# Five rotating banks, an earlier place for the routing matmuls and nine lead units in a routed feed-forward kernel

## What is computed

```python
idx, w = _route(xf, Wr, br)                      # 6 of 32 experts per row, weights w
gate = jnp.zeros((T, E), w.dtype).at[jnp.arange(T)[:, None], idx].add(w)

def step(acc, ew):
    w1, w2, g = ew
    h = jnp.square(jax.nn.relu(xf @ w1.T)) @ w2.T
    return (acc + g[:, None] * h, None)
acc, _ = jax.lax.scan(step, jnp.zeros_like(xf), (W1, W2, gate.T))
shared = jnp.square(jax.nn.relu(hidden_tensor @ Ws1.T)) @ Ws2.T
return shared + moe_out
...
x = x + s * g                                    # g = silu(shared + moe_out)
```

## Time and profile before

| | |
|---|---|
| median of three timed runs | 337.94 us (333.05, 337.94, 338.01) |
| profiled execution | 335.13 us, span 333.3 us |
| TensorE busy | 297.5 us, 89% of the span |
| VectorE, ScalarE, GpSimd busy | 229.0, 179.3, 208.0 us |
| mean granted TensorE clock | 0.968 of full speed |
| gathers of rows, issue to landing, median | 3.3 us |
| gathers of slots' results | 66 by 0.98 us |

### The profile page before, as it was taken

The page is one execution under the profiler, slowest core; times in us unless marked ns, Lnnn a source line. Parts: engine busy times, 40 slices in busy tenths (PEclk is TensorE's granted clock), DMA queues, the critical chain, the costliest instruction groups (busy, mean ns, idle before and its releaser), DMA issues.

```text
span 333.3 us, 6927 instructions
## 1 busy us (share of the span) xinstructions
PE 297.5 (89%) x2224; PEld 231.8 (70%) x2224; DVE 229.0 (69%) x585; ACT 179.3 (54%) x293; POOL 208.0 (62%) x226
## 2 busy tenths in 40 slices
PE   0577899879997999999999999998999999995994
PEld 0344666547776977888888698885767767785893
DVE  3788678887631378677778767687767576753774
ACT  3888598695452755557665576653363331212322
POOL 1874656681577777777777777304666777774640
PEclk9997899989997999999999999999999999995999
DMA  7455746722463376676766767555688777666552
GB/s 283 188 176 190 239 146 244 283 94 63 104 180 116 108 222 204 201 204 207 219 203 194 219 196 210 183 173 192 181 327 259 220 197 212 189 182 163 147 154 79
DMA packets 39651, 62.92 MB, mean 189 GB/s; under 512 B 5282, under 2 KB 25538, under 8 KB 39618
## 3 DMA queue, kind: packets, MB, share of 16 engines
q1 hardware_dynamic: 31794, 41.11, 37.2%
q0 software_dynamic: 7824, 21.38, 23.4%
HBM read 46.13 MB, written 16.33 MB: 187 GB/s over the span
## 4 chain that ended last, share of the span: by engine, by line
PE 56%; DMA 15%; POOL 8%; DVE 7%; ACT 6%; issue 6%; DVEq 1%; ACTq 0%
PE rot L962 12%; PE dp L990 10%; DMA yk<-ytab,slot 10%; PE rot L915 5%; PE hp L939 4%; DMA xgt<-xtab,ids 4%; POOL xgt L614 4%; PE hp L951 3%; PE hp L953 3%; PE hp L952 3%; POOL yk L623 3%; PE hp L941 3%; PE hp L940 3%; PE rot L975 2%; DVE xs L1265 2%
## 5 line engine op out<-in xcount | busy, mean ns | idle before, releaser
L614 POOL DMA_INDIRECT xgt<-xtab,ids x97 | 96.4, 994 | 39.7 <-issue 21.3
L680 ACT ACTIVATE hf<-hf 128x512 f32<-128x512 f32 (+2 forms) x74 | 45.8, 619 | 98.7 <-DVE hf L1246 74.8
L623 POOL DMA_INDIRECT yk<-ytab,slot x66 | 64.7, 980 | 44.3 <-DMA ytab<-late 17.1
L990 PE MATMUL dp<-w2s,hf 128*128 128x256 f32 x340 | 83.6, 391 | 4.3 <-issue 4.3
L990 PEld LDWEIGHTS dp<-w2s,hf 128*128 128x128 f32 x340 | 66.1, 198 | 16.2 <-issue 4.7
L694 ACT ACTIVATE xgt<-rot 128x1024 f16<-128x1024 f16 (+1 forms) x49 | 49.3, 1009 | 9.6 <-PE rot L915 9.2
L962 PE MATMUL rot<-w2s,hf 128*128 x194 | 51.3, 391 | 1.1 <-ACT xgt L694 1.0
L953 PE MATMUL hp<-xh,wlo 128*128 128x512 f16 (+2 forms) x148 | 45.0, 322 | 0.0
L952 PE MATMUL hp<-xh,whi 128*128 128x512 f16 (+2 forms) x148 | 45.0, 322 | 0.0
L951 PE MATMUL hp<-xh,whi 128*128 128x512 f16 (+2 forms) x148 | 44.9, 321 | 0.0
L1265 DVE SCALAR_TENSOR_TENSOR xs<-yk,wk,xs 128x256 f32<-128x256 f32 x66 | 32.0, 484 | 16.8 <-DMA yk<-ytab,slot 14.8
(11 more groups left out here) (162 smaller groups left out, 473.5 us busy)
## 6 DMA issues: line engine op xcount, KB each, us to landing
ytab<-late SPq DMA_DIRECT2D x48, 256.0 KB, 2.8
gate_bc<-gtab SPq DMA_DIRECT2D x40, 256.0 KB, 3.8
late<-in_w SPq DMA_DIRECT2D x17, 256.0 KB, 4.9
w2s<-in_w SPq DMA_DIRECT2D x8, 512.0 KB, 6.4
xs<-in_x SPq DMA_DIRECT2D x4, 512.0 KB, 4.7
xgt<-in_x SPq DMA_DIRECT2D x4, 512.0 KB, 6.5
out<-xgt SPq DMA_DIRECT2D x16, 128.0 KB, 3.7
xgt<-xtab,ids POOLq DMA_INDIRECT x97, 3.3
```

The source lines that it names most:

```text
L614: nc.gpsimd.indirect_dma_start(xg[:, a % XRING, :], None, xtab, bass.IndirectOffsetOnAxis(ids[:, a:a + 1], 0))\
L623: nc.gpsimd.indirect_dma_start(yk[:, n % KRING, :], None, ytab, bass.IndirectOffsetOnAxis(slot[:, n // K, n % K:n % K + 1], 0))\
L990: mm = nc.tensor.matmul(dp[:, q // 2, q % 2, :], hf[:, k % HRING, cols], w2s[:, e, :], start=(e == 0 and q % 2 == 0), stop=(e == N - 1), s ...
```

## The change

1. The two banks of `dp` become banks 3 and 4 of `rot`. After the lead units, ScalarE copies chunk 0's sum so far to `acc` (`leave_lead`), and from then on five banks go round in the slots. The sum starts anew behind the slots and is at the end added to `acc` on DVE (`leave_sum`), not copied on ScalarE.
2. `place` stands one unit earlier and behind `first(k)`: k = 8 to 13. DVE's splits of the last weights stay at units 14 to 16.
3. Chunk 1's weights (`weigh(1)`) go from behind the second one-hot to unit 19, its root to behind the gathers, and its turn, copy and store to units 44 and 45.
4. `LEAD` is 9: the slots are units 17 to 41, and 23 dense units of chunk 0 follow them. Block 1 still begins at unit 65. Everything counted from the slots (branch, adds, finishes of routed tiles) comes one unit earlier.

```diff
-LEAD = 10
+LEAD = 9
...
-        rot = bank("rot", [P, 3, 2, D])
-        dp = bank("dp", [P, 2, 2, D])
+
+        rot = bank("rot", [P, 5, 2, D])
+        dp = rot[:, 3:5]
...
+        lead_last, lead_end = EARLY + LEAD - 1, NS + LEAD
...
-        PLACE_AT = HOT_AT + 1
+        PLACE_AT = HOT_AT
...
-        GATES_AT = [4, PLACED - 1][0:len(BLOCKS)]
+        GATES_AT = [4, EARLY + LEAD + GROUPS + 2][0:len(BLOCKS)]
...
-        use_no = {use: n for n, use in enumerate(uses)}
-        bank_of = {use: n % 3 for n, use in enumerate(uses)}
+
+        JOIN = uses.index(("turn", EARLY + LEAD + 3, 0)) + 1
+        bank_of, user_before, last_user = {}, {}, {}
+        for n, use in enumerate(uses):
+            b = n % 3 if n < JOIN else (3, 4, *[(JOIN + i) % 3 for i in range(3)])[(n - JOIN) % 5]
+            bank_of[use], user_before[use], last_user[b] = b, last_user.get(b), use
...
         def wait_bank(engine, *use):
 
-            n = use_no[use]
-            if n < 3:
+            if user_before[use]:
+                wait_left(engine, user_before[use])
+            elif bank_of[use] >= 3:
+                engine.wait_ge(lead_out, 2)
+            else:
...
             for s in range(1, POOL_STEPS):
                 low_w(s)
-                if s == POOL_STEPS - 3:
-                    for b in range(1, len(BLOCKS)):
-                        gate_root(b)
...
                   .then_inc(xg_landed[a % XRING], 16)
+            for b in range(1, len(BLOCKS)):
+                gate_root(b)
...
+            def leave_lead():
+                act.wait_ge(lead_done, 1)
+                for h, own in enumerate(pairs_of(dense_tiles(BLOCKS[0]))):
+                    nc.scalar.activation(acc[:, own[0]:own[-1] + 1, :], dp[:, h, 0:len(own), :], ACT.Copy)\
+                      .then_inc(lead_out, 1)
...
-                for c in BLOCKS:
+                if k == lead_last + 2:
+                    leave_lead()
+                for c in BLOCKS[1:]:
                     if k == last_of[c] + 3:
                         leave_sum(c)
...
+                if u == lead_end and c == BLOCKS[0]:
+                    for b in (3, 4):
+                        wait_left(pe, last_user[b])
+                ends = (lead_end - 1, N - 1) if c == BLOCKS[0] else (N - 1,)
+                starts = (0, lead_end) if c == BLOCKS[0] else (0,)
...
-                if 0 <= k - PLACE_AT < len(HOT_PAIRS):
-                    place(HOT_PAIRS[k - PLACE_AT])
...
+                if 0 <= k - PLACE_AT < len(HOT_PAIRS):
+                    place(HOT_PAIRS[k - PLACE_AT])
                 kind = UNITS[k - 2][0]
...
+            def leave_sum(c):
+                dve.wait_ge(sum_done, BLOCKS.index(c) + 1)
+                if c == BLOCKS[0]:
+                    dve.wait_ge(lead_out, 2)
+                for h, own in enumerate(pairs_of(dense_tiles(c))):
+                    o = acc[:, own[0]:own[-1] + 1, :]
+                    nc.vector.tensor_tensor(o, dp[:, h, 0:len(own), :], o, ALU.add).then_inc(sum_out, 1)
...
                     relu(HOT_AT + i // 2)
-                if i == 1:
-                    weigh(1)
...
+                if k == last_of[BLOCKS[0]] + 3:
+                    leave_sum(BLOCKS[0])
```

More of the change, by code:

```diff
@@ L292, in build @@
         sum_done = sem("sum_done")
+        lead_done = sem("lead_done")
+        lead_out = sem("lead_out")
         sum_out = sem("sum_out")
@@ L419, in build, with wait_left @@
             uses += [("leave", i, h) for i in leaving(k) for h in range(i != LAST, len(leaves[i]))]
-        use_no = {use: n for n, use in enumerate(uses)}
-        bank_of = {use: n % 3 for n, use in enumerate(uses)}
-        def wait_bank(engine, *use):
-            n = use_no[use]
-            if n < 3:
+        JOIN = uses.index(("turn", EARLY + LEAD + 3, 0)) + 1
[3 more added lines that the diff above has]
+            bank_of[use], user_before[use], last_user[b] = b, last_user.get(b), use
+        def wait_left(engine, use):
+            what, k, h = use
+            if what == "turn":
+                engine.wait_ge(xt_copied, leaves[k][h][-1] + 1)
+            else:
+                wait_y(engine, store_no[k, h])
+        def wait_bank(engine, *use):
+            if user_before[use]:
+                wait_left(engine, user_before[use])
+            elif bank_of[use] >= 3:
+                engine.wait_ge(lead_out, 2)
+            else:
                 engine.wait_ge(shared_out, len(shared_no))
                 engine.wait_ge(eoff_ready, 1)
-                engine.wait_ge(gt_ready, len(BLOCKS))
-            else:
-                what, k, h = uses[n - 3]
-                if what == "turn":
-                    engine.wait_ge(xt_copied, leaves[k][h][-1] + 1)
-                else:
-                    wait_y(engine, store_no[k, h])
+                engine.wait_ge(gt_ready, 1)
         @block.sync
@@ L725, in silu_sum @@
                     act.wait_ge(rows_ready, f - 1)
+                elif f == 0:
+                    act.wait_ge(gt_stored, 16 * len(BLOCKS))
                 nc.scalar.activation(tz[:, f % 2, :], acc[:, j, :], ACT.Silu).then_inc(tz_ready, 1)
@@ L798, in _ @@
                     high_w(s)
-                if k == PLACE_AT:
+                if k == PLACE_AT + 1:
                     act.wait_ge(branch_landed, 16 * 5)
@@ L990, in second_dense @@
                         mm = nc.tensor.matmul(dp[:, q // 2, q % 2, :], hf[:, k % HRING, cols], w2s[:, e, :],
-                                              start=(e == 0 and q % 2 == 0), stop=(e == N - 1), skip_group_check=True)
+                                              start=(e in starts and q % 2 == 0), stop=(e in ends), skip_group_check=True)
+                if k == lead_last:
+                    mm.then_inc(lead_done, 1)
                 if k == last_of[c]:
@@ L1372, in _ @@
                 for s in range(POOL_STEPS, WSTEPS):
-                    if k == PLACED - 1 + (s - POOL_STEPS) // 2:
+                    if k == PLACED + (s - POOL_STEPS) // 2:
                         low_w(s)
-                for c in range(2, NCH):
+                for c in range(1, NCH):
                     if k == WEIGH_AT(c):
```

2 lines of the change are left out of this document (1 added, 1 removed).

## The result

| | before | after |
|---|---|---|
| median of the timed runs | 337.69 us (333.05 to 338.01, 4 runs) | 342.53 us (341.66 to 344.73, 4 runs) |
| profiled execution, span | 335.13 us, 333.3 us | 341.66 us, 339.9 us |
| mean granted TensorE clock | 0.968 | 0.968 |

The changed kernel is slower by the ratio 1.0256, 95% interval 1.0196 to 1.0317. A second set of runs further down gave 1.0188 (1.0125 to 1.0252). The ratios leave out runs that were more than 1.5% above the fastest of their kernel, the medians take in all. By the medians the change costs 4.8 us, 1.4%, in both sets. So it is slower for certain, and over 2% only perhaps. I had forecast 339.0 us and "within 2%" as the likeliest.

What follows compares the result with a forecast made beforehand. It took the 97 gathers to bound the slots and TensorE the stretch behind them; 1.8 + 3.0 - 1.6 - 0.5 = +2.7 us gave 337.8 on the profiled execution or 340.6 on the median, so 339.0 us, range 333.0 to 345.0.

Steps and rivals of the forecast that it cites:

- What bounds the stages: Slots: 97 gathers set their length, ending 139.1 us after the ids, TensorE some 1 us behind the last row at most.
- Five banks, -0.5 us: Slots: five banks instead of three only cut TensorE's lag behind the last gather, between 0 and 1 us, taken as -0.5.
- Nine lead units, +3.0 us: Ahead of the slots: the dense unit taken off becomes idle time and is paid behind the slots, +3.0 us.
- Gate root behind the gathers, nothing: GpSimd: chunk 1's 10.1 us of small operations hide in 17.06 us of idle time behind the gathers; nothing saved.
- Placement behind the first layer, +1.8 us: Placement stretch: the new order delays the shared second layer, ids at 87.2 to 88.1 instead of 85.88, taken as +1.8 us.
- the relu's wait of about 1 us: Placement: one new wait, about 1 us, as DVE's relu of unit 11 comes later and the next one-hots are behind it.
- The 0.5 us of the last relu: End of the placement: the last relu must also pass before the ids, 0.5 us.
- the 12.5 us: Third placement to the last: three first layers and three second layers in both orders, 12.5 us as before.
- The stop before block 1, -1.6 us: TensorE before chunk 1's first sum: with the sum on DVE the stop shrinks from 4.3 to 2.9 us, -1.6 us.
- The number between 337.8 and 340.6: Forecast time 339.0 us, put between the sum added to the profiled execution and the sum added to the timed median.
- Placement gets quick: Rival, faster: if DVE is kept fed, ids come up to 7.4 us earlier, 329.8 us in all; chance 0.06.
- Starved TensorE loses its clock: Rival, slower: waits for rows in the slots bring the low clock, 5.7 to 24 us longer, up to 363; chance 0.07.

Runs made afterwards that it cites:

- after2: The changed kernel itself, unaltered, measured once more in a later set of runs: 341.6 us, ratio 1.0188 to the kernel before.
- l_only: The kernel before with nine lead units instead of ten and nothing else changed: 340.31 us, ratio 1.0098 to the kernel before.
- bg_only: The changed kernel with the old placement and ten lead units, keeping five banks, the sum on VectorE and the gate move: 332.6 us, ratio 0.9897 to the kernel before.
- after_no_p: The changed kernel with the old placement put back, still nine lead units: 337.0 us, ratio 0.9983 to the kernel before.
- bg_ten: The same kernel as bg_only, with ten lead units, measured again in a later set: 332.49 us, ratio 0.9853 to the kernel before.
- l11c: bg_only with eleven lead units instead of ten, measured beside bg_ten: 328.41 us, ratio 0.9756 to the kernel before.
- bg_l11: bg_only with eleven lead units, in the sets where every kernel took some 35 us more: ratios 0.9888 and 0.9871 to the kernel before.

## Why the prediction was wrong, step by step

**What bounds the stages: right.** In the fourteen traces of the table the 97 gathers took 122.7 to 124.9 us from first to last, whatever else was changed, and the slots ended 138.5 to 141.5 us behind the first. An id that is late makes the end late. But the gathers end some microseconds before the slots do: the last turn stood 5.05 to 7.88 us behind the last gather's start. I had put TensorE at most 1 us behind the last row, from the shortest of these.

**Five banks, -0.5 us: right in that they gain nothing, wrong in size.** The profiled E - G rose by 1.8 us, and this misses the term by as much as the placement misses its own. after2 has 139.2, and over all traces five banks have 1.0 us more than three, so the size differs from one execution to the next. I had taken one execution's 139.1 us as a constant; it varies by some 2 us. The waits did go over from banks to rows, as I had it: "DMA" ended a wait of the turns' matmuls or weight loads 11 times instead of five. Whether the banks themselves lengthen the stage stays open.

**Nine lead units, +3.0 us: right.** By the ratios 3.3 us in l_only, 2.9 between bg_only and after_no_p, -3.3 between bg_ten and l11c. In l_only, where the copy stays on ScalarE, the stop before block 1 shrank by 0.5 us only (3.84 instead of 4.30).

**Gate root behind the gathers, nothing: right on GpSimd, wrong on VectorE.** The root is hidden; it took 8.09 us more than its operations, and the first gather of the adds still waited 6.07 us for a store. But its weights stood in the chain of the one-hots. I had written that they leave the one-hots, and let them count only within the new placement. Alone they are worth 2.1 us of placement, 3.7 with the slow stretch that followed their stop in before and not in l_only.

**Placement behind the first layer, +1.8 us: the step that failed.** The order of events was as I stepped it: shared layer from 64.83 (forecast 64.2 to 65.1), ScalarE's link from its end to the third placement 5.2 us (5.1), TensorE idle 3.02 us (3.7) ahead of that placement, the relu's wait of about 1 us (0.80). What was wrong is the length of the shared layer itself. I held it back behind a waiting TensorE and still gave it its old 3.5 us at full clock. It took 5.2 us at the lower level, behind stops of 0.67 and 1.56 us. From the first placement on, the third came after 15.7 us (13.0 to 13.9 by my bounds) and the first gather after 30.8 (27.7 to 28.6): of the 2.2 us beyond my upper bound 1.7 are this clock.

The rest is my adding up. The 0.5 us of the last relu, which I name, is not in the 87.2 to 88.1: 72.8 + 12.5 + 1.0 and the 0.85 us from the last placement to the ids make 87.2 already. With it the upper bound is 29.1, and that is what after2 shows, whose shared layer kept the full clock behind the same stops. These are its rows:

```profile
67.84 0.44 PE L922 MATMUL bp<-xgt 128*128 128x98 f16 x6 [1.56 <-ACT xgt L697]
68.12 3.68 PE L997 MATMUL rot<-w2s,hf 128*128 128x256 f32 x16
```

The second slow stretch, behind the stop of 3.02 us, was no miss: the 12.5 us that I took over from before hold that execution's own slow stretch, 1.6 us (26.4 against 24.8 in l_only).

The frame hid how much was at stake. I counted from the 26.4 us of one execution of before. Against the 22.7 us to which the gate move had brought it, the new placement costs 6.4 to 8.1 us. So my +1.8 was the net of a gain of up to 3.7 us that I had called nothing and of a cost that I never priced by itself.

**The stop before block 1, -1.6 us: right.** 2.58 instead of 4.30 us on TensorE. (My "2.9" for the stop was a slip; 4.3 less 1.6 is 2.7.) VectorE's sum ends it: it is done at 310.64, and TensorE starts at 310.74. The profile names ScalarE's square, but that was done at 310.10. The slow clock behind it stayed, as I had kept it. VectorE's row and the stretch:

```profile
309.36 1.28 DVE L1295 TENSOR_TENSOR xs<-rot,xs 128x512 f32<-128x512 f32 x2
...
312.00:314.00 2.00, 2.00 (x19) 1.86 (x18) 0.18 (x1) 0.00 (x0) 1.39 (x3) 0.50 0.82 265
```

With the lead unit's +3.0 this gives 109.7 us behind E; measured 109.1 and 107.4. In after2, with the 107.4, no slow stretch followed the stop.

**The sum.** Forecast +1.8 + 3.0 - 1.6 - 0.5 = 2.7; by the traces +4.06 in the placement, +1.8 in the slots, +0.8 behind them, 6.6. The number between 337.8 and 340.6 was a fair base: 339.0 and the missing 3.9 us are 342.9, and the median is 342.5. Of the 3.9 us, 2.3 were missing in the placement and 2.3 in the slots, and 0.6 too much stood behind them. Only the placement's share is explained by the experiments.

**The rivals.** "Placement gets quick" did not come, though bg_only shows its mechanism: with the weights off VectorE and the old order, the first gather is at 82.40. "Starved TensorE loses its clock" did not come either. From 120 to 300 every stretch of 10 us in the changed kernel shows a granted clock of 1.00; one of the slots':

```profile
200.00:210.00 10.00, 8.77 (x78) 1.00 0.68 205
```

The waits for rows were 3.2 us in all, the longest 1.2 us. The Trainium skill (TensorE: Matmul & The Clock Gate, section "HAM oscillation — how this bites in real kernels") tells of bursts of matmuls that are shorter than the waits for transfers between them, with the low clock back at each. Here a unit's matmuls take some 4.4 us and the waits 0.4 to 1.2, so this is not the case that it describes, and my "by that rule this rival would come true" went too far.

What came ahead of a low clock in the changed kernel were longer stops (3.02 us ahead of 76, 2.65 ahead of 116, 2.58 ahead of 312) or three short ones close together (0.58, 0.67 and 1.56 us between 59 and 65). But the length of a stop does not settle it. These stops, one each of after2, bg_only and l_only, were followed by a clock of 1.00:

```profile
310.89 1.10 PE L1017 MATMUL rot<-w2s,hf 128*128 128x256 f32 x4 [2.59 <-ACT hf L692]
...
111.16 0.66 PE L937 MATMUL rot<-cst,xgt 128*128 128x128 f32 x4 [2.82 <-ACT xs L727]
...
74.90 0.44 PE L900 MATMUL bp<-xgt 128*128 128x98 f16 x6 [1.65 <-ACT xgt L685]
```

Of the nine stops at the first lent bank in the traces of the table (2.65 to 2.87 us) six were followed by a stretch of 2 us at 0.50 to 0.55, three kept 1.00. What decides between them is not shown.

## What to carry to other kernels

A wait that is moved ahead of another work item also moves everything that hangs on that item: look at who consumes it, here ScalarE's 5 us of copies, and price the new stop with and without the lower clock behind it. For the same stop both were measured here, 1.7 us apart in the shared layer. Before costing a new order, ask for each engine in the chain which instruction could leave it altogether; moving 1.6 us of small operations out of the chain of one-hots gained some 2 us, and none of the reorderings tried here gained anything in time. And where a fixed stage (here 97 gathers) follows filler work, give the filler as many units as the ring of buffers can hide: from nine to ten and from ten to eleven units the time fell by some 3 us each.

## What the runs showed of the hardware

**A start that is 1 or 3 us late.** bg_only and bg_ten are the same kernel, and S is 59.66 in one and 62.65 in the other. First bg_only's rows, of VectorE and TensorE, and a stretch:

```profile
48.15 0.22 DVE L1353 CAST ntf<-cnt 32x128 f16<-32x128 int32 x1
48.42 0.18 PE L909 MATMUL bp<-tri,ntf 32*128 32x32 f16 x1 [0.75 <-DVE ntf L1353]
...
50.00:52.00 2.00, 2.00 (x10) 1.25 (x10) 1.85 (x12) 1.06 (x3) 0.01 (x1) 1.00 0.16 60
```

and these are bg_ten's, with GpSimd's split:

```profile
48.45 1.16 POOL L582 TENSOR_TENSOR wlo<-late,whi 128x512 f16<-128x512 f32 x1 [2.37 <-ACT whi L666]
48.80 0.89 DVE L1353 CAST ntf<-cnt 32x128 f16<-32x128 int32 x1
49.74 0.18 PE L909 MATMUL bp<-tri,ntf 32*128 32x32 f16 x1 [1.42 <-DVE ntf L1353]
...
50.00:52.00 2.00, 2.00 (x6) 1.63 (x6) 1.71 (x8) 0.00 (x0) 0.00 (x0) 0.50 0.28 94
```

Of the 3.0 us, 1.3 stand before 50: in bg_ten a short cast on VectorE falls into GpSimd's split (the next paragraph is on such meetings), takes 0.89 us instead of 0.22, and TensorE stops for 1.42 us instead of 0.75. The other 1.7 are the low clock behind this. All eighteen traces fall into three groups: five have the short cast, no low clock at 50 to 54 and S at 59.3 to 59.8; thirteen have the long one, and of these five keep the clock (S 60.4 to 60.7) and eight do not (62.5 to 63.0). The thirteen, and only they, had also been at the low level between 38 and 44. So up to 3 us of the difference between two executions fall ahead of everything that was changed here. What decides the clock at either place stays open.

**VectorE beside GpSimd.** In the changed kernel GpSimd's splits and VectorE's one-hots (the rows at 73.00 and 74.65 above) met. These are the split at 61.89 and the two at 72 to 76, one by one:

```profile
61.89 1.16 POOL L582 TENSOR_TENSOR wlo<-late,whi 128x512 f16<-128x512 f32 x1 [2.40 <-ACT whi L666]
...
72.12 1.98 POOL L582 TENSOR_TENSOR wlo<-late,whi 128x512 f16<-128x512 f32 x1 [9.08 <-ACT whi L666]
...
74.06 1.68 POOL L582 TENSOR_TENSOR wlo<-late,whi 128x512 f16<-128x512 f32 x1
```

The one-hot that began at 73.00 ended at 74.72, 0.6 us behind the end of the first split; the next, from 74.65, ended at 76.56, 0.8 behind the end of the second. The two splits lost time too, 1.98 and 1.68 us instead of 1.16: the second met a one-hot under way, the first began together with another (72.14) that took its usual 0.95 us. The Trainium skill (SBUF — State Buffer, section "SBUF: two separate sides") says that the port pair they share is an exclusive lock: the operation that starts first has it for its whole length, and the other fully blocks. Among the VectorE operations it counts those with two inputs in SBUF, against a GpSimd operation that reads SBUF. The trace agrees with the blocking; which of the two was first at 72.12 and 72.14 it can't tell.

**GpSimd behind its gathers.** The first operation of the gate root after the last gather was followed by 8.09 us of idle time without a releaser, the same in every variant that has it there (8.1). It is hidden here; in a chain it would count.

**Two sets of runs at another level.** In two sets all kernels took some 35 us more: 371.25 us for the one before, with clocks of 0.96 to 0.97. In G - S nothing differs. The slots take 23 to 26 us more and the rest of the span 9 to 16 us more than in the same kernels elsewhere. In the slots TensorE rests up to 1.1 us again and again without a releaser, and GpSimd waits for it; waits of the two in the run bg_l11, up to 225:

```profile
PE hp L963 <- issue: 3.7, 5, 1.0
...
POOL xgt L624 <- PE rot L937: 20.5, 16, 2.2
```

Where these pauses come from was not found.
